# Two graph layers on one core: one slot product per tile, types of two groups at once, a placing product, and index loads for four groups

## The reference, cut to what matters

```python
h = jnp.maximum(_layernorm(x), 0.0)
# layer 0: per edge h[src] @ weight[type], summed by destination
for r in range(16):
    msg = msg + h_src * (etypes == r)[:, None] @ weight[r]
x = x + segment_sum(msg, dst)
h = jnp.maximum(_layernorm(x), 0.0)
# layer 1: per edge a small two-layer network, summed by destination
msg_input = concatenate([h[src], h[dst], edge_attr], axis=1)
msg = relu(msg_input @ W1 + b1) @ W2 + b2
x = x + segment_sum(msg, dst)
```

## Time and profile before

| | us |
|---|---|
| median of 3 runs | 5445.96 (5436.07 to 5465.1) |
| the profiled execution | 5515.39 |
| its span, first to last instruction | 5513.6 |
| PE busy | 3026.3 (55%) |
| POOL busy | 3156.1 (57%) |
| DVE busy | 1329.3 (24%) |
| ACT busy | 721.8 (13%) |

### The profile page before, as it was taken

One profiled execution on the slowest core, in us unless ns is written; L12 is line 12 of the kernel. 1 busy time (PEld: TensorE's weight loads), 2 busy tenths in 40 slices (PEclk: granted clock), 3 DMA queues, 4 the chain that ended last, 5 costly groups with the idle time before them and its releaser, 6 DMA issues.

```text
span 5513.6 us, 63778 instructions
## 1 busy us (share of the span) xinstructions
PE 3026.3 (55%) x19447; PEld 2533.6 (46%) x19447; DVE 1329.3 (24%) x2774; ACT 721.8 (13%) x1445; POOL 3156.1 (57%) x3343
## 2 busy tenths in 40 slices
PE   2455554555555455455545655556556556655566
PEld 2334443444344344343434555555555555555555
DVE  6222322233232233232411111111111111111111
ACT  2010111111111011111111111111111111111111
POOL 7555555555555655555355555555555555555554
PEclk9666666666666667666766766667667766676677
DMA  4111111111111111111011111111111111111111
GB/s 92 21 24 23 22 24 22 22 24 22 23 24 22 23 24 23 22 23 24 19 25 25 27 26 27 26 27 26 27 26 26 26 28 25 26 27 26 26 27 23
DMA packets 247902, 144.26 MB, mean 26 GB/s; under 512 B 178328, under 2 KB 194001, under 8 KB 247873
## 3 DMA queue, kind: packets, MB, share of 16 engines
q0 software_dynamic: 106496, 109.26, 10.5%
q1 hardware_dynamic: 138734, 34.02, 3.0%
q10 hardware_dynamic: 2642, 0.63, 0.1%
HBM read 129.98 MB, written 12.83 MB: 26 GB/s over the span
## 4 chain that ended last, share of the span: by engine, by line
PE 44%; issue 38%; another core or an unknown queue 10%; DVE 3%; DVEq 1%; ACT 0%; ACTq 0%
PE ps L1197 10%; PE ps L1205 9%; PE ps L1138 7%; PE ps L1147 7%; PE ps L1188 4%; PE ps L1195 4%; DVE acc L997 2%; DVE onehot L933 1%; PE ps L1176 1%; PE ps L1118 1%; PE ps L1186 1%; DVEq L997 0%; DVEq L990 0%; PE ps L1107 0%
## 5 line engine op out<-in xcount | busy, mean ns | idle before, releaser
L615 POOL DMA_INDIRECT rows<-p_table,idx x1664 | 1569.6, 943 | 1221.6 <-DMA idx<-in_src_dram 687.8
L615 POOL DMA_INDIRECT rows<-h_table,idx x1616 | 1529.6, 947 | 1091.3 <-DMA idx<-src_tab 616.1
L1197 PE MATMUL ps<-q_win,onehot_t 128*128 128x64 f32 x3328 | 593.0, 305 | 907.7 <-issue 906.3
L1197 PEld LDWEIGHTS ps<-q_win,onehot_t 128*128 128x128 f32 x3328 | 585.1, 237 | 1049.3 <-issue 1049.1
L1138 PE MATMUL ps<-onehot,rows 128*64 128x128 f32 x6656 | 769.0, 349 | 498.5 <-issue 456.8
L1147 PE MATMUL ps<-slots,w_pairs 128*64 128x128 f32 x3328 | 634.5, 329 | 610.4 <-issue 594.0
L1138 PEld LDWEIGHTS ps<-onehot,rows 128*64 128x64 f32 x6656 | 578.5, 178 | 649.7 <-issue 597.2
L1147 PEld LDWEIGHTS ps<-slots,w_pairs 128*64 128x64 f32 x3328 | 494.7, 169 | 729.8 <-issue 708.4
L997 DVE TENSOR_TENSOR acc<-acc,ps 64x16 f32 x1664 | 272.6, 164 | 1794.1 <-remote 945.3
L1205 PE MATMUL ps<-onehot,relus 128*65 128x128 f32 x3328 | 561.0, 338 | 57.7 <-issue 56.7
L1205 PEld LDWEIGHTS ps<-onehot,relus 128*65 128x65 f32 x3328 | 512.0, 180 | 62.5 <-issue 61.2
(11 more groups left out here) (99 smaller groups left out, 721.7 us busy)
## 6 DMA issues: line engine op xcount, KB each, us to landing
rows<-p_table,idx POOLq DMA_INDIRECT x1664
rows<-h_table,idx POOLq DMA_INDIRECT x1616
attr<-in_edge_attr_dram SPq DMA_DIRECT2D x209, 32.0 KB
q_win<-q_table SPq DMA_DIRECT2D x208, 32.0 KB
idx<-in_src_dram SPq DMA_DIRECT2D x208, 4.0 KB
idx<-src_tab SPq DMA_DIRECT2D x202, 4.0 KB
p_table<-pq_out SPq DMA_DIRECT2D x25, 120.0 KB
q_table<-pq_out SPq DMA_DIRECT2D x25, 120.0 KB
```

The lines of the kernel that those rows point to most:

```text
L615: pool.indirect_dma_start(rows[:, u, t, :], None, table, bass.IndirectOffsetOnAxis(ap=idx[:, u, t:t + 1], axis=0)).then_inc(s, 16)
L1197: last = pe.matmul(pre_ps[:, u % 2, j * D:(j + 1) * D], onehot_t[:, u % 2, j * P:(j + 1) * P], q_win[:, u % V, :], start=False, stop=(j == ...
```

## The change

Loads of indices. `idx` is loaded for four groups at a time (`B = 4`) in both layers: a load waits until all four groups that used these slots are through, and POOL waits once for four groups. In layer 1 `attr` is also loaded for four groups, and `q_win` for two.

Layer 0. The key is 16 times the type plus the offset, over 256 columns. There is one product per tile, of 256 columns, and tiles of even and odd number write the two halves of the PSUM partitions. ACT copies the slots into an order by type. The types of two groups are applied at once: 16 products, whose weights are the slots of 128 (tile, offset) pairs and whose moving operand is `w_types`, a block matrix with the type's weight twice. ACT copies the result (`copy_nodes`), and a new product with a one-hot matrix `place` (made by DVE, `make_place`) puts it at its nodes of two windows of 128. DVE adds two windows for two groups, in place of sixteen.

Layer 1. The transposed one-hot matrix isn't made by PE any more. Destination keys are stored as bytes in a table in DRAM, loaded with the same row in all 128 partitions (`key_rows`, 512 KB for four groups), and compared by DVE with the partition's number. Of the transposes that of the attributes stays. Several waits that others imply are gone.

```diff
-    PAR = 2
-    RP = R // PAR
+    B = 4
-    C0 = RP * W0
+    C0 = R * W0
...
-                def group(it, u):
-                    g = it * U + u
-                    wait_apart(sp, slots_summed, 2 * (g + 1))
-                    sp.dma_start(idx[:, u, :], src_tab[:, bass.ds(g, 1), :]).then_inc(idx_in[u], 16)
+                def batch(it, k):
+                    g = it * U + k * B
+                    wait_apart(sp, slots_summed, 2 * (g + B))
+                    sp.dma_start(idx[:, k * B:(k + 1) * B, :], src_tab[:, bass.ds(g, B), :]).then_inc(idx_in[k], 16)
...
+                def pairs(it, first=False, last=False):
+                    for n in range(U // 2):
+                        m = it * (U // 2) + n
+                        if not first or n >= 2:
+                            wait_apart(sp, pre_added, AHEAD + 2 * m - 2)
+                        if n == 1 and not first:
+                                load_idx(it * U + B, 1)
+                                load_attr(it * U + B, 1)
+                                load_keys(it * U + B, 1)
+                        if n == 3 and not last:
+                            load_idx((it + 1) * U, 0)
+                            load_attr((it + 1) * U, 0)
+                            load_keys((it + 1) * U, 0)
+                        load_q(it, n)
...
                     for u in range(U):
-                        wait_apart(pool, idx_in[u], 16 * (it + 1) if u >= EG else 16 * it)
+                        if u % B == 0:
+                            wait_apart(pool, idx_in[u // B], 16 * (it + u // B))
                         for t in range(T):
                             gather(h_table, u, t, rows_in[u])
...
-                    for t in range(T):
-                        window = acc[0:D, bass.ds(bases[t], W0)]
-                        dve.wait_ge(window_added, AHEAD * T + g * T + t)
-                        dve.tensor_tensor(window, window, node_ps[:, b, t * W0:(t + 1) * W0], ALU.add).then_inc(window_added, 1)
+                    for b in range(2):
+                        window = acc[0:D, bass.ds(bases[b], W1)]
+                        if b == 1:
+                            dve.wait_ge(window_added, AHEAD + 2 * m + 1)
+                        dve.tensor_tensor(window, window, win_ps[:, b * W1:(b + 1) * W1], ALU.add).then_inc(window_added, 1)
...
+                    dve.tensor_scalar(onehot_t[:, u % 2, :], key_rows[:, u, :], node_f[:], None, ALU.is_equal).then_inc(onehot1, 1)
...
                     for t in range(T):
-                        for par in range(PAR):
-                            last = pe.matmul(slot_ps[par * D:(par + 1) * D, b, t, :], rows[:, u, t, :],
-                                             onehot[:, b, t, par * C0:(par + 1) * C0], start=True, stop=True)
+                        last = pe.matmul(slot_ps[t % 2 * D:(t % 2 + 1) * D, b, t // 2, :], rows[:, u, t, :], onehot[:, b, t, :], start=True, stop=True)
...
+                def apply_types(m, b):
+                    pe.wait_ge(slots_copied, 4 * (m + 1))
+                    for r in range(R):
+                        last = pe.matmul(nodes_ps, slots[:, b, r, :], w_types[:, r, :], start=(r == 0), stop=(r == R - 1))
+                def place_nodes(m):
+                    pe.wait_ge(nodes_copied, m + 1)
+                    pe.wait_ge(place_made, m + 1)
+                    for h in range(2):
+                        last = pe.matmul(win_ps, nodes_t[:, h * D:(h + 1) * D], place[:, h, :], start=(h == 0), stop=(h == 1))
...
-                    pe.transpose(attrt_ps, attr[:, u % V, :], ident[:])
-                    for j in range(T):
-                        last = pe.transpose(oht_ps[:, j * P:(j + 1) * P], oh1[:, u % 4, j, :], ident[:])
+                    pe.transpose(attrt_ps, attr[:, u, :], ident[:]).then_inc(group_turned, 1)
```

More of the change, by code:

```diff
@@ L43, in gnn_kernel @@
     W1N = P
-    C0 = RP * W0
+    C0 = R * W0
+    W1 = P
+    NP = G // 2
+    T2 = T // 2
+    Q = 2 * T2
     CP, CI = 120, 4
@@ L58, in gnn_kernel @@
     EG = 6
-    NWL = 2 + 1 + 4 + T + 3
+    NWL = 2 + 4 + T + 3
     PG = 2
@@ L225, in gnn_kernel @@
         blocks_cleared = sem("blocks_cleared")
-        idx_in = [sem(f"idx_in_{u}") for u in range(U)]
+        idx_in = [sem(f"idx_in_{h}") for h in range(U // B)]
         rows_in = [sem(f"rows_in_{u}") for u in range(U)]
@@ L254, in gnn_kernel @@
         q_in = [sem(f"q_in_{u}") for u in range(V)]
-        attr_in = [sem(f"attr_in_{u}") for u in range(V)]
+        attr_in = [sem(f"attr_in_{h}") for h in range(U // B)]
+        key_in = [sem(f"key_in_{h}") for h in range(U // B)]
+        tail_in = sem("tail_in")
         onehot1 = sem("onehot1")
@@ L415, in tile @@
                         r = slice(half * R // 2, (half + 1) * R // 2)
-                        last = pe.matmul(ps[:, 2 + half, :], s_gt[0:D, :], w_all[:, r, :].rearrange("k r m -> k (r m)"), start=True, stop=True)
+                        last = pe.matmul(ps[:, 2 + half, :].rearrange("p (r m) -> p r m", m=D), s_gt[0:D, :], w_types[0:D, r, 0:D], start=True, stop=True)
                 else:
@@ L581, in _, with idx_of, attr_of @@
-                for u in range(U):
-                    group(0, u, first=True)
-                for u in range(U):
-                    group(1, u)
-                with sp.Fori(2, NIT) as it:
-                    for u in range(U):
-                        group(it, u)
+                def idx_of(edges, n):
+                    return src[edges].rearrange("(g p j) -> p g j", p=P, j=T)
+                def attr_of(edges, n):
+                    return edge_attr[edges, :].rearrange("(g p j) f -> p g (j f)", p=P, j=T)
@@ new lines, in load_q @@
+                def load_q(it, n):
+                    m = it * (U // 2) + n
+                    _, bases = nc.values_load_multi_w_load_instructions(
+                        base_row[0:1, bass.ds(2 * m, 2)], engines=[ENG.SP], min_val=0, max_val=N - 1,
+                        skip_runtime_bounds_check_because="dst holds nodes' numbers")
+                    for b in range(2):
+                        slot = (2 * n + b) % V
+                        sp.dma_start(q_win[:, slot, :], q_table[bass.ds(bases[b], P), :]).then_inc(q_in[slot], 16)
@@ L588, in _ @@
+                sp.wait_ge(bytes_stored, 16)
+                for k in range(U // B):
+                    load_keys(k * B, k)
+                    load_attr(k * B, k)
+                pairs(0, first=True)
+                pairs(1)
+                with sp.Fori(2, NIT - 1) as it:
+                    pairs(it)
                     store_out(it - 2, chunk_nodes)
+                store_out(NIT - 3, chunk_nodes)
+                pairs(NIT - 1, last=True)
                 store_out(NC - 1, chunk_nodes)
-                sp.wait_ge(attr_in[G % V], 16 * (G // V + 1))
+                sp.wait_ge(key_in[0], 16 * (NIT + 1))
@@ L1004, in step @@
                             (add_sums, sum_squares, make_h)[u - 5](it - 1, chunk_nodes)
-                        add_windows(k - 1, (u - 1) % 2)
+                    if u % 2 == 1:
+                        m = it * (U // 2) + u // 2
+                        if not first or u >= 3:
+                            add_windows(m - 1)
+                        make_place(m)
+                dve.wait_ge(key_copied, 1)
                 for u in range(U):
@@ L1133, in sum_slots @@
                         pe.wait_ge(h_made_a, NA + u // PG + 1)
+                    if u % 2 == 0 and (not first or u >= 2):
+                        wait_apart(pe, slots_copied, 2 * (g - 1))
                     pe.wait_ge(onehot0, g + 1)
```

289 lines of the change are left out of this document (173 added, 116 removed).

## The result

The changed kernel took 5784.71 us in the median of 4 runs (5775.32 to 5789.89), the kernel before 5455.53 (5436.07 to 5467.04, 4 runs): the ratio is 1.0605, with a 95% interval of 1.0567 to 1.0644. It is 6% slower. The forecast was 5390 us, 1% faster, and the range up to 5760 misses it by 25 us. The profiled execution has a span of 5784.8 us.

What follows compares the result with a forecast made beforehand. POOL's gathers and waits for indices, with PE nearly standing still in long runs, were taken as the bound. Layer 0 -18, layer 1 -31, first wait -5: 5515 - 54 = 5461, times 0.9874 gives 5390 us; range 5100 to 5760.

Steps and rivals of the forecast that it cites:

- POOL's waits for indices bound the kernel: POOL's gathers in both layers: 1304 us in 216 waits for indices, which would become about 102 of 11 to 13 us.
- 62 MATMULs in the first 9 us of a run: PE at the beginning of a run of gathers: some 60 products in 9 us, as in the earlier trace.
- 88 MATMULs within 42.2 us: PE during a run of 32 gathers: 62, 22 and 4 MATMULs, leaving 53 and 56 for behind it.
- The step that failed: PE behind a run of 32: remaining MATMULs take 9.3 us in layer 0, 9.8 in layer 1; 51.5 and 52.0 in all.
- The 2.5 us: PE behind a run's last gather: its pace comes back 2.5 us later, at 42.2 us for 32 gathers.
- The wait behind the first 64 gathers: POOL's 29.07 us wait there would shrink by about 5 us, with five groups worked off at 4.45 us.
- Rival D: POOL's run length alone sets the wait, some 15.6 us behind 32 gathers: +311 us, median 5750 us; chance 0.32.
- my case: Both layers: the main forecast, -54 us and a median of 5390 us, own range 5290 to 5490; chance 0.45.
- Rival B: Slow stretches share a fixed amount among all engines, so fewer DVE and SP instructions help PE: -285 us, median 5165; chance 0.17.
- C: The standstill does not come, POOL never waits and the 1304 us go: median 4160 us; chance 0.06.
- DVE's comparison: Layer 1's byte comparison beside POOL's gathers: 0 to +92 us, taken as 0.
- The parts that I set to 0: DVE's windows, ACT's copies, dropped waits, key loads and preparation: 0 us each, the preparation within 10.

Runs made afterwards that it cites:

- e2: Kernel before, with POOL alone waiting for the indices of four groups ahead of every fourth group, so runs of 32 gathers: 6219.13 us, 1.1254 of the kernel before.
- e3: Changed kernel, with POOL also waiting behind each group's 8 gathers until these have landed: 5143.89 us, 0.9313 of the kernel before.
- e9: Changed kernel, unchanged, run again in a block without the standstill: 4284.63 us against 4218.40 for the kernel before, ratio 1.0156.
- g1: Kernel before, with POOL also waiting ahead of each group until the rows of the group two back have been used: 5268.52 us, 0.9642 of the kernel before.

## Why the prediction was wrong, step by step

- That POOL's waits for indices bound the kernel, that runs become 32 gathers long (39.7 us) and that the waits become about 102: right (39.7 to 39.8 us, 100 waits).
- 62 MATMULs in the first 9 us of a run: right (65 and 59).
- 88 MATMULs within 42.2 us: right in layer 0 (65.8 + 16.9 + 6.8 = 89.5), 8 too many in layer 1 (80.4). The even spread that I took from the earlier trace rows isn't there; that its sum held in layer 0 is luck.
- **The step that failed: "Layer 0: 6.1 us give 27, the other 26 take 3.2 us: 42.2 + 9.3 = 51.5 us", and for layer 1 "26 in 6.1 us, 30 in 3.7: 42.2 + 9.8 = 52.0".** That is PE's recovery behind the run, at 5.7 MATMULs a us from 42.2 us on. Measured are 51.3 in 11.06 us (4.6 a us) and 63.6 in 14.71 (4.3). I let PE run from 2.5 us behind the last gather on. It starts some 3 us later (4.5 and 1.7 MATMULs from 42.2 to 45.2 us), and only then has a pace like mine, 5.8 a us in layer 0 and 5.3 in layer 1. The 2.5 us were those of runs of 16 and 24; behind a run of 32 the others come back later. What they come back from is the late signal shown above (ACT's copy at 1163.03 in the run at 1120, 3.3 us behind its last gather): the prediction had a late start of 2.5 us as a fixed term, without a reason for it. Why the signals come late stays open.
- In us: a run and its wait take 53.3 and 56.9 in these averages, not 51.5 and 52.0. In layer 0 all of the 1.8 us is the late start. In layer 1, 63.6 MATMULs at my pace would be 11.1 us: of the 4.9 us, 1.3 are the 8 MATMULs more, 3.6 the late start and the pace. Over the layers, with a group at 13.27 and 14.11 us by the page instead of 12.88 and 13.0, it is 0.39 x 202 + 1.11 x 208 = 310 us, which leads from 5461 to 5771; the profiled execution has 5786.5. The wait behind the first 64 gathers shrank by 2.6 us (29.07 to 26.4), where I had 5.
- Rival D had the size (waits of 15.6 us; measured 15.3 in the mean) with a reason that is half right: the length of the run sets the scale of the wait (e2), but fewer products do shorten it, from 19.6 to 15.3 us (two blocks). Its words that signals between engines, not PE's own work, are what comes late fit the 47% of the chain that the changed kernel spends on such waits, and ACT's copies that start 11.3 us behind their products. It got 0.32 where my case had 0.45. The earlier trace rows held two of its three points.
- Rival B, a shared fixed amount, isn't borne out as I priced it (waits of 9 or 10 us), and C was thrown out by the wrong argument. The standstill does go with a small edit (e3), and in some blocks it isn't there: the kernel before took 4218 us in two blocks, close to the 4160 that I worked out for "no standstill". But the change is not what removes it.
- DVE's comparison: the prediction took 0 of 0 to 92 us, "since a POOL that is held a little later waits less". With the standstill the gathers lengthened by 1585.5 - 1569.6 = 16 us, and no more showed. Without it, it is 57 us, 0.27 for each of 208 comparisons. A rule of the Trainium skill (SBUF — State Buffer, section "SBUF: two separate sides") says that DVE's use of both ports keeps POOL from writing descriptors. The trace agrees in kind: 1.27 against 0.94 us beside it, and 943 ns with the operand in PSUM. In size, a comparison held POOL for its whole length (0.80 us) would have cost 167 us; a third of it was measured.
- The parts that I set to 0 on PE, DVE and SP (placing product, windows, dropped waits, key loads) make no wait of their own in e9: there POOL waits for indices once (14.8 us, as layer 0 begins). Beside a standstill they weren't separated.

## What to carry to other kernels

Where one engine issues long strings of indirect DMAs, look at what the others do in each 5 us of the string before you batch what feeds it: a wait that looks like overhead may be the break that lets the others work. Where there was a standstill, limiting the lead of the gathering engine was worth 3.6% (g1), and joining its waits by four cost 12.5% (e2). Arrears are not worked off at an engine's free pace from the moment the stop ends: count what comes in the first us behind a stop of that length, and keep a term for it when the length is one that no row shows. And time a change in more than one place if something outside the program may be part of it: the same edit was +6.1% and +1.6%. Look whether the profile is complete (are landing times missing in part 6, does the chain name an unknown queue?) before you build on it, and time the kernel without the profiler as well, which wasn't done here.

## What the runs showed of the hardware

- In the block of the result the engines answered each other late: ACT's copies began 11.3 us behind the products that they waited for in the mean of 416 (changed kernel), 0.14 us in e3, with the pauses, and 0.04 us in e9, without a standstill.
- With the gathers running one every 1.25 us, PE and DVE can come to issue nothing for 22 us (x0 at 1140.00 to 1162.20), although DMA's share is 0.14 there. Gathers keep their 0.94 us. It was seen in recorded executions only.
- A pause of 2.2 us behind each 8 gathers ended the waits that come of this (e3), the same behind each 16 didn't (969 us left), and 0.7 us behind each 8 ends only part of them (1105 left of 1532).
- In two blocks of runs it was absent: the kernel before took 4218 us (4217.1 to 4220.4 in 14 runs), the same program that took 5446 to 5522 us elsewhere. The traces with it lack 61 to 79% of the DMAs' signals, those without it under 1%. Which resource stands behind it, whether the recording is part of it, and why it is there in one place and not in another, stays open.
- A tensor_scalar of 128x1024 bytes to fp32 took 0.76 to 0.80 us on DVE, the tensor_tensor with PSUM 1.21; beside the first, gathers of 0.94 us took up to 1.27 us in the lines shown, 0.27 us more for each comparison in the mean of e9; beside the second they kept their 943 ns.
